# A six-stage fp32 decoder on one core: large SBUF tensors begin at multiples of 256 bytes, and more idle products stand in front of the norms' first tiles

## What is computed

```python
x = x + attention(layernorm(x), Wq, Wk, Wv, Wo)            # a0: 16 heads of 32, causal
x = x + cross_attention(layernorm(x), ctx, mask)           # m: 1024 context rows, weights-free
x = x + mixture(layernorm(x), ...)                         # f0: 16 experts, top 6, 2 shared, 352 inner, gated
x = x + attention(rms(x) * w, w_in, w_out, rotary)         # a1: 32 query heads of 64, 8 groups of keys and values, causal
x = x + linear_attention(layernorm(x), ctx, Wq.., Wqf..)   # lin: relu features, 16 heads, biases
x = x + mixture(layernorm(x), ...)                         # f1: 8 experts, top 2, 1 shared, not gated
```

## Time and profile before

| what | value |
|---|---|
| median of three runs | 1957.86 us |
| profiled execution, its own time | 1941.73 us |
| its span | 1940.3 us |
| instructions | 30,576 |
| busy: TensorE, VectorE, ScalarE, GpSimd | 93%, 57%, 42%, 52% |
| DMA | 232.52 MB, mean 120 GB/s |

### The profile page before, as it was taken

One profiled execution on the slowest core, in us unless ns is written; L12 is line 12 of the kernel. 1 busy time (PEld: TensorE's weight loads), 2 busy tenths in 40 slices (PEclk: granted clock), 3 DMA queues, 4 the chain that ended last, 5 costly groups with the idle time before them and its releaser, 6 DMA issues. The chain is left out here.

```text
span 1940.3 us, 30576 instructions
## 1 busy us (share of the span) xinstructions
PE 1805.5 (93%) x10047; PEld 1564.1 (81%) x10053; DVE 1111.9 (57%) x2769; ACT 806.8 (42%) x2063; POOL 1009.6 (52%) x965
## 2 busy tenths in 40 slices
PE   6999989999699999999779999999999999998996
PEld 4888857788699999899658888888888888866796
DVE  5676785673233333335766666666666756565445
ACT  3767643222122222221256656566565433553232
POOL 3444342387773957995456546456453203115783
PEclk7999989999899999999899999999999999999999
DMA  3556430246543645554343234233331210011666
GB/s 108 161 165 202 142 136 2 75 154 226 198 168 121 214 160 179 177 174 120 88 109 103 66 94 106 63 88 97 80 75 55 73 41 9 23 49 60 218 218 196
DMA packets 104550, 232.52 MB, mean 120 GB/s; under 512 B 20672, under 2 KB 20928, under 8 KB 101328
## 3 DMA queue, kind: packets, MB, share of 16 engines
q1 hardware_dynamic: 84080, 144.31, 24.8%
q0 software_dynamic: 19744, 85.47, 13.6%
q10 hardware_dynamic: 576, 0.79, 0.1%
HBM read 126.23 MB, written 57.93 MB: 95 GB/s over the span
## 5 line engine op out<-in xcount | busy, mean ns | idle before, releaser
L706 POOL TENSOR_SCALAR a_E<-a_E,a_inv 128x128 f32<-128x128 f32 (+3 forms) x384 | 220.0, 592 | 226.9 <-DVE a_inv L842 226.9
L153 PE MATMUL bank<-f_UH,f_XH 128*128 x596 | 201.2, 338 | 23.0 <-POOL f_UL L165 18.0
L739 ACT ACTIVATE a_E<-a_E,a_top 128x512 f32<-128x512 f32 (+3 forms) x384 | 211.1, 567 | 6.7 <-DVE a_top L836 6.6
L153 PE MATMUL bank<-f_UH,f_XL 128*128 x596 | 193.4, 324 | 0.0
L153 PE MATMUL bank<-f_UL,f_XH 128*128 x596 | 193.3, 324 | 0.0
L731 ACT ACTIVATE a_PHL<-bank 128x512 fp32r<-128x512 f32 (+1 forms) x288 | 130.7, 528 | 133.4 <-PE bank L1016 133.4
L836 DVE CUSTOM_DVE_ANT_0 a_E<-a_causal,bank 128x512 f32<-128x512 bf16 (+3 forms) x384 | 163.8, 482 | 30.3 <-PE bank L1000 18.5
L153 PE MATMUL bank<-a_PHL,a_VH 128*128 128x512 f32 (+3 forms) x768 | 180.8, 324 | 0.3 <-DVE a_QL L165 0.3
L1827 DVE TENSOR_TENSOR f_gate<-bank,f_gate 128x352 f32<-128x352 f32 x79 | 41.4, 524 | 207.5 <-PE bank L153 207.4
L165 DVE TENSOR_TENSOR a_PHL<-bank,a_PHL 128x512 fp32r<-128x512 f32 (+1 forms) x288 | 153.8, 588 | 11.2 <-ACT a_PHL L731 11.1
L1772 ACT ACTIVATE f_HH<-bank 128x256 fp32r<-128x256 f32 x220 | 59.9, 324 | 234.4 <-PE bank L2169 234.3
(11 more groups left out here) (407 smaller groups left out, 4869.8 us busy)
## 6 DMA issues: line engine op xcount, KB each, us to landing
f_uraw<-f_up POOLq DMA_DIRECT2D x18, 1408.0 KB, 6.7
f_xb<-table SPq DMA_DIRECT2D x86, 256.0 KB, 3.4
table<-f_ob SPq DMA_DIRECT2D x86, 256.0 KB, 2.8
table<-a_zeros SPq DMA_DIRECT2D x31, 512.0 KB, 4.5
f_draw<-f_down POOLq DMA_DIRECT2D x27, 512.0 KB, 4.5
a_g<-a_f SPq DMA_DIRECT2D x160, 64.0 KB, 2.0
a_raw<-a_qkv SPq DMA_DIRECT2D x36, 256.0 KB
f_uraw<-f_up POOLq DMA_DIRECT2D x9, 704.0 KB, 4.5
```

The costliest lines, as they stand in the source:

```text
L153: m = pe.matmul(out, a, b, start=first and i == 0 and j == 0, stop=last and i == n - 1 and j == 2, skip_group_check=not check)
L706: e.tensor_scalar(self.E[sl][:, a], self.E[sl][:, a], self.inv[:, sl, i:i + 1], 0.0, ALU.mult, ALU.add).then_inc(*self.s_nrm.up(N, m - 1, i))
L739: x = e.activation(E, E, ACT.Exp, scale=-1.0, bias=self.top[:, sl, i:i + 1], accum_out=self.total[:, sl, i:i + 1])
```

## The change

**1. The order of the declarations in SBUF.** `stats` and `full` and 160 bytes that nobody uses (`to_line`) go in front of X, and in every stage the small tensors go behind the large ones. Nothing that is computed or moved changes. The start of a tensor, modulo 256 bytes:

| tensors | before | after |
|---|---|---|
| X; YH, YL | 128; 64 | 0; 0 |
| ident, identb | 64 | 0 |
| a0 and a1: WH, WL, raw, QH, QL, VH, VL, E, PHL and the key tensors | 96 | 0 |
| a0: zeros; a0 and a1: f, g, causal | 32 | 0 |
| m: CH, CL, RH, RL, mb; E, PH, PL | 96; 128 | 0; 0 |
| m: the norm's tiles | 192 | 0 |
| f0 and f1: UH, UL, DH, DL, raw weights, rows, XH, XL, gate | 96 | 0 |
| f0 and f1: HH, HL | 224 | 0 |
| lin: W1, W2, raw, features, CH, CL, KH, KL, kf | 96 | 0 |
| lin: kvH; kvL; rows and pick | 160; 32; 160 | 0; 128; 0 |
| lin: vHL, two buffers | 0 and 128 | 0 and 128 |

A row of UH or UL has 352 columns, 1,408 bytes, so every second row begins at 128 past its tensor's start, before and after. All stages end within SBUF.

**2. Idle products.** `pe_mingled` issues 19 where it had 9, `pe_half` 24, `pe` 22. In the second attention alone (the one with a rotary table) idle products come into `Attention.pe`: six in bank 7 ahead of the first loop; 18 in bank 4 at loop 0 ahead of the fill; 5, 4 and 7 in bank 4 at loops 1, 2 and 3, behind the scores. Those in bank 4 wait until it is empty. In the Linear stage nine go into bank 0 ahead of the context of the second batch, after a wait for that bank.

```diff
-    def warm(self, n):
+    def warm(self, n, bank=7):
...
-            self.pe.matmul(self.bank[7][:, :], self.identb[:, :], self.identb[:, :].rearrange("p (a c) -> p a c", a=1).broadcast_to(
+            self.pe.matmul(self.bank[bank][:, :], self.identb[:, :], self.identb[:, :].rearrange("p (a c) -> p a c", a=1).broadcast_to(
...
     def pe_mingled(self):
-        self.k.warm(9)
+        self.k.warm(19)
...
     def pe(self, then=None):
         e, lag = self.k.pe, 2
-        self.k.warm(9)
+        self.k.warm(22)
...
     def pe_half(self):
-        self.k.warm(9)
+        self.k.warm(24)
...
         self.norm.pe_half()
+        idle = {self.begin: 6, 0: 18, 1: 5, 2: 4, 3: 7} if self.rotary is not None else {}
         for m in self.loops:
+            if m < 0:
+                self.k.warm(idle.get(m, 0))
+            elif m == 0 and m in idle:
+                e.wait_ge(*emptied[self.SR])
+                self.k.warm(idle[m], self.SR)
             if m == 0 and self.rotary is not None:
                 self._pe_fill(m, emptied)
             if 0 <= m < self.M:
                 self._pe_scores(m, emptied)
+            if m > 0 and m in idle:
+                e.wait_ge(*emptied[self.SR])
+                self.k.warm(idle[m], self.SR)
             if 2 <= m < self.M + 2:
                 self._pe_transposes(m - 2, emptied)
...
         if b == 0 and h == 0:
             e.wait_ge(*self.s_wlo_pool.after("k", KD - 1))
         else:
+            if b and h == 0:
+                e.wait_ge(*emptied[0])
+                self.k.warm(9, 0)
             self._context_split(e, b, h)
...
-        k.X, k.stats = k.sb("X", [NT, D]), k.sb("stats", [NT, 6])
+        k.stats, k.full, _ = k.sb("stats", [NT, 6]), k.sb("full", [7]), k.sb("to_line", [40])
+        k.X = k.sb("X", [NT, D])
...
-        self.top, self.total, self.inv = (sb(x, [self.SLOTS, 4]) for x in ("top", "total", "inv"))
...
+        self.top, self.total, self.inv = (sb(x, [self.SLOTS, 4]) for x in ("top", "total", "inv"))
...
-        self.mb, self.valid, self.ones = sb("mb", [B, SC], BF16), sb("valid", [B]), sb("ones", [P], BF16)
+        self.mb, self.ones = sb("mb", [B, SC], BF16), sb("ones", [P], BF16)
...
-        self.top, self.total = sb("top", [NT, 2]), sb("total", [NT, 2])
+        y = [sb(f"y{i}", [D])[:, :] for i in range(4)]
+        self.top, self.total, self.valid = sb("top", [NT, 2]), sb("total", [NT, 2]), sb("valid", [B])
...
+        self.HH, self.HL = sb("HH", [3, P], F32R), sb("HL", [3, P], F32R)
         self.gate = sb("gate", [INNER])
-        self.HH, self.HL = sb("HH", [3, P], F32R), sb("HL", [3, P], F32R)
```

More of the change, by code:

```diff
@@ L91, in constants @@
         self.ones, self.earlier = self.sb("ones", [P], BF16), self.sb("earlier", [P], BF16)
-        self.upto, self.full, self.number = self.sb("upto", [16, 16]), self.sb("full", [7]), self.sb("number", [64])
+        self.upto, self.number = self.sb("upto", [16, 16]), self.sb("number", [64])
         self.s_zeros, self.s_cleared, s_ones = self.event("zeros"), self.event("cleared"), self.event("ones")
@@ L1065, in __init__ @@
         self.ma, self.mf = sb("ma", [B, SC], U8), sb("mf", [SC])
-        self.mb, self.valid, self.ones = sb("mb", [B, SC], BF16), sb("valid", [B]), sb("ones", [P], BF16)
+        self.mb, self.ones = sb("mb", [B, SC], BF16), sb("ones", [P], BF16)
         self.E = [sb(f"E{i}", [SC]) for i in range(2)]
         self.PH, self.PL = [sb(f"PH{i}", [SC], F32R) for i in range(2)], [sb(f"PL{i}", [SC], F32R) for i in range(2)]
-        self.top, self.total = sb("top", [NT, 2]), sb("total", [NT, 2])
+        y = [sb(f"y{i}", [D])[:, :] for i in range(4)]
+        self.top, self.total, self.valid = sb("top", [NT, 2]), sb("total", [NT, 2]), sb("valid", [B])
         self.nb, self.inv = sb("nb", [NT]), sb("inv", [NT])
-        self.norm = Norm(k, "m", lambda nm, shape: sb(f"n_{nm}", shape), banks=list(range(NT)))
+        self.norm = Norm(k, "m", lambda nm, shape: sb(f"n_{nm}", shape), y, banks=list(range(NT)))
         sig = lambda x: k.event(x, "m")
@@ L2313, in __init__ @@
         self.F = {x: (sb(f"F{x}H", [self.G * FD], F32R), sb(f"F{x}L", [self.G * FD], F32R)) for x in "kq"}
-        self.bq, self.bk, self.bv, self.bo = sb("bq", [KD]), sb("bk", [KD]), sb("bv", [D]), sb("bo", [D])
-        self.am = sb("am", [CT])
+        self.bv, self.bo = sb("bv", [D]), sb("bo", [D])
         self.CH, self.CL = sb("CH", [KD, SC], F32R), sb("CL", [KD, SC], F32R)
@@ L2319, in __init__ @@
         self.kfH, self.kfL = ([sb(f"kf{x}{i}", [HN * FD], F32R) for i in range(2)] for x in "HL")
-        self.v = sb("v", [HN, VA])
         with ExitStack() as same:
@@ L2324, in __init__ @@
         self.vHL = [sb(f"vHL{i}", [2, HN, VA], F32R) for i in range(2)]
+        self.kvH, self.kvL = sb("kvH", [B * NP, 2 * VA], F32R), sb("kvL", [B * NP, 2 * VA], F32R)
+        self.rows = [sb(f"rows{i}", [T], F32R) for i in range(2)]
+        self.pick, self.pickraw = sb("pick", [P], F32R), sb("pickraw", [P])
         self.acc = sb("acc", [B * NP, 2 * VA])
+        self.v = sb("v", [HN, VA])
         self.zerob = sb("zerob", [3 * 4 * VA], BF16)
-        self.kvH, self.kvL = sb("kvH", [B * NP, 2 * VA], F32R), sb("kvL", [B * NP, 2 * VA], F32R)
+        self.bq, self.bk, self.am = sb("bq", [KD]), sb("bk", [KD]), sb("am", [CT])
         chunks = lambda c: c[:, :, :].rearrange("p k (a t) -> p (k a) t", t=T)
@@ L2333, in __init__ @@
         self.den = [self.kf[FD:FD + 2, :], craw1[FD:FD + 2, :, :].rearrange("p a t -> p (a t)")]
-        self.rows = [sb(f"rows{i}", [T], F32R) for i in range(2)]
-        self.pickraw, self.pick = sb("pickraw", [P]), sb("pick", [P], F32R)
         self.rden = sb("rden", [2, 32])
```

## The result

The changed kernel takes 1943.34 us (median of ten runs, 1934.85 to 1951.8) where the kernel before took 1954.86 beside it (ten runs, 1949.21 to 1965.44). The ratio is 0.9934, with a 95% interval from 0.9914 to 0.9954: 12.9 us faster (1,955 times 0.0066; the two medians differ by 11.5). The forecast was faster by 76 us, with 1882 as the time.

What follows compares the result with a forecast made beforehand. TensorE was taken as the bound. Layout 73.6 plus 12 us, times 0.82, gave 70; idle products 6; together 76 off 1941.7 is 1865.7, forecast as 1882 because the profiled execution lay under the median; range 1862 to 1954.

Steps and rivals of the forecast that it cites:

- What bounds the kernel: Whole kernel: TensorE, busy 93% of the span, sets the end; GpSimd, at 52%, is next in line.
- 0.82: Share of TensorE's saving reaching the end: all of it in two windows (39% of matmuls), 0.7 elsewhere; bounds 0.55 and 1.
- The sum, layout: Wide fp32r products at full clock: 6,815 steps save 10.8 ns each, 73.6 us; with 12 us for unlike offsets, 85.6 us.
- the block of 128 bytes: Moving operands beginning between 128-byte lines touch one block more per row, 13.33 ns per product; aligned starts remove it.
- Rival N: Wide fp32r products are slow by nature and the address costs nothing: 6 us off, 1952; chance 0.17.
- The second term, like offsets: 2,543 512-wide steps with unlike operand offsets save 3.4 to 6.2 ns each, 9 to 16 us, taken as 12.
- Case A of the rivals: Only like offsets of the two operands matter: 16 us off, 1942; chance 0.13.
- the forecast case: Layout and idle products together save 76 us, time 1882, own range 1862 to 1912; chance 0.60.
- Rival C: Operands all beginning on one line hinder each other, 6.2 ns more per 512-wide step: slower, 1970; chance 0.04.
- rival S: The layout gives nothing; idle products run at half clock, 427 ns each, and outlast their gaps: slower, 1976; chance 0.06.
- The sum of 6 us: Idle products before norms, in the second attention's loops and the Linear stage: 7 us gained, less 1 for tiles that slip.
- the windows in which TensorE never pauses: Stretches 533.5 to 776 and 1018.5 to 1455 us, holding 39% of matmuls, where all of TensorE's saving was to count.

Runs made afterwards that it cites:

- The trains: The changed kernel with trains of 24 like products behind its last stage, widths and operand starts varied; like 512-column pairs at multiples of 32 stepped at 226.7 to 227.8 ns.
- the third set: The changed kernel with trains copying the mixtures' down product behind its last stage; 226.7 ns with 128 rows, 228.8 with 128, 128 and 96, 233.4 with weights 128 bytes further.

## Why the prediction was right or wrong

**What bounds the kernel** held. A saving on TensorE's path reached the end: the wide steps became 2.5 ns shorter, 3,517×2.5 = 8.8 us, and the layout alone is worth 0.0059, 11.5 us, with an interval of some ±0.2% (4 us) for each of its comparisons. How much of it passes through isn't measured: 8.8×0.82 = 7.2 us lies inside two of the three intervals and below the mean, and the mean is more than even 1 would give. GpSimd didn't become the bound of the whole.

**The step that failed is "The sum, layout", its 73.6 us for the block of 128 bytes**: nothing of it was there (352 columns stepped at 160.0 and then 159, like operands of 512 columns at 226.5 and then 229). I had three spacings, 226.7, 160.0 and 120.0, and read them as 17/16, 12/11 and 9/8 of the columns' time. But N columns fill N/32 blocks of 13.33 ns, so one block more is 13.33 ns more at any width. The three ratios were one number in three dresses, and a fixed price for each product fits them exactly as well. Rival N named that ("by nature") and I gave it 0.17, dismissing it because the excess "grows by bytes", which it did not, and because it vanishes at the half clock, which a fixed price could do too, if a slower stream hides it (not shown). The 384 and 128 columns that the forecast counts for N tell nothing between the two, since both give 173.3 and 66.7 ns; the 60 ns at 128 speaks against both. No width could have decided it, and no wide operand of that trace began at 0 modulo 128; a train at two starts was needed. The trains decide: 226.7 at 0 and 227.8 at 96.

By the Trainium skill, "TensorE: Matmul & The Clock Gate", section "Back-to-back issue gap", an isolated warm product is spaced by N/2.4+2.5 ns, about 216 at 512 columns, and the columns N are the only term; the section's own figure for a sustained stream, about 131 ns, is lower. The bf16 train agrees with the 216 (216.3) and not with the 131; the fp32r trains take 10.4 ns more than the 216 at best. By the Trainium skill, "SBUF — State Buffer", section "SBUF: two separate sides", TensorE never waits on anyone on its port. Whether another engine makes it wait can't be seen in trains in which nothing else runs; what they show is that its own two operands, when unlike, cost it up to 6.5 ns at 512 columns.

**The second term, like offsets, was the right mechanism** with about the right size: 3.4 to 6.2 ns on 2,543 steps, 12 us of TensorE's work taken, 8.8 measured. It is shown by the memory stage from both sides, 227.3 and 226.8 with all alike at 0 and at 96, and 233 and 226.4 in one stage with YH and YL moved alone. Too high was the count: 885 of the steps called unlike are the mixtures' down products, which gained 1 ns, not 5. Case A of the rivals, 16 us off, is what happened (12.9); it had 0.13. That 1943 lies inside the stated 1862 to 1954 is owed to the stretch over the rivals; the forecast case's own range ended at 1912. Rival C is refuted by the same rows.

**The idle products** did in the trace what the working says, norm by norm: the first mixture's norm (first idle product to first product) went from 9.56 to 7.99 us (1.5 expected), the first attention's from 16.43 to 15.13 (0.7), the second attention's from 13.70 to 12.85 (0.5), the last mixture's from 9.67 to 8.00 (0.8, but there all kernels with the new layout and nine had 7.99 as well), the memory stage's from 15.33 to 15.33 (0.5): VectorE paces its tiles, as the gaps of 0.70 and 1.40 in front of its next tiles show, and the 24 idle products run right up to the first tile at 252.87. The clock did stay up during them, against rival S; not throughout, since the first mixture's 19 took 4.28 us, 216 ns each, and the first attention's 24 took 8.16, 338 each. The sum of 6 us lies between the 8 measured alone and the 1 to 2 on top of the layout. Why it shrinks there isn't settled. In single profiles the low stretches vary from one to the next: they add up to 106 and 116 us in those of before, 68 and 65 in the changed kernel's, 75 with the idle products alone, but 123, 92 and 85 in three with the layout alone. Over all runs the granted clock shows more: its mean is 0.970 in the kernel before (20 runs) and 0.971 with the layout alone (8), against 0.977 with the idle products alone (12), and later 0.971 (27) and 0.972 (9) against 0.978 in the changed kernel (11). So the idle products raise the clock by 0.006 to 0.007 with either layout, an estimated 20 to 30 us less at the low level (twice the difference, times the span). The effect on the clock doesn't shrink; the time that it brings does.

**One cover not seen.** In the first mixture TensorE waits for GpSimd's low part of the next weights whenever it is early. The rows of before and after:

```profile
521.79 0.65 PE L153 MATMUL bank<-f_UH,f_XH 128*128 x1 [14.96 <-POOL f_UL L165]
```

```profile
512.93 0.66 PE L153 MATMUL bank<-f_UH,f_XH 128*128 x1 [9.30 <-POOL f_UL L165]
```

That wait ends 142 and 141 us after the mixture's first product, and 139 to 142 us after it in all eight profiles that have it; its end is GpSimd's. What TensorE saves ahead of it within the mixture should then only be waited longer. The lengths don't test that, since they follow the clock as well: 14.96 and 5.79 us in the two profiles of before, 9.30 and 8.61 in the changed kernel's, and none over 0.9 us in seven others, which all had low stretches earlier in the mixture. I had read only the windows in which TensorE never pauses, and took 0.7 for all of the rest; that this cover cost the change anything isn't shown.

## What to carry to other kernels

Lay the moving operand and the weights of wide fp32r products so that their starts are equal modulo 256 bytes, at a multiple of 32; which multiple doesn't matter. It was worth 6 ns of 233 at 512 columns, 1 ns in the mixtures' down products, and nothing from 448 columns down. Before a model is fitted to several sizes, write it as a difference too: if the excess is the same number at each size, the sizes don't tell a block from a fixed price, and a train of like products at two starts does. Idle products in front of a norm pay where the gap is real and the next tile isn't paced by another engine, 1 to 2 us each here; whether several of them add up has to be measured together.

## What the runs showed of the hardware that was not expected

- With like operands and 128 columns of weights, fp32r products of 256 to 416 and of 512 columns took 13 to 15 ns beyond the columns' own time at the full clock (226.7 at 512), 480 and 448 columns 17 to 20. Narrower weights took no less (230 to 232 at 512). The bf16 products took 3 (216.3).
- Unlike starts (by 16 to 128 bytes) cost 2 to 7 ns at 512 columns and nothing that shows from 448 down.
- A moving operand that begins 4 bytes past a multiple of 256 took 237.7 ns with the weights at 4 too and 237.0 with the weights at 0, more than any other pair with 128 columns of weights. Both at 16 gave 230.1. With 32 columns of weights, 32 bytes off, it was 240.1.
- In a train of 32 rows without a pause the granted clock fell. The window of TensorE over that train (length, busy, clock, DMA share, GB/s):

```profile
2070.10:2077.90 7.80, 7.80 (x25) 0.69 0.00 0
```

TensorE was busy for all of 7.80 us and the clock averaged 0.69. In the third set a train of 72 such products averaged 364 ns, ending at 0.5, where trains of 64 and of 96 rows kept 1.0.
